# A graph kernel with an LSTM over windows: six pieces of the last layer write into the other stream's F bank

## What is computed

```python
def _L0_gnn_ref(x, adj, Wg0, bg0, Wg1, bg1, Wih, Whh, bih, bhh):
    h = relu(einsum('ts,bsh->bth', adj, x @ Wg0 + bg0))
    h = relu(einsum('ts,bsh->bth', adj, h @ Wg1 + bg1))
    for p in range(1, 5):
        nw = T // p
        last = _lstm_last(Wih[p-1], Whh[p-1], bih[p-1], bhh[p-1], h[:, :nw*p].reshape(B*nw, p, H))
        h = h.at[:, arange(nw)*p + p-1, :].set(last.reshape(B, nw, H))
    return h

def _L1_gnn_ref(x, W, adj, bias):
    h = einsum('bjf,kfo->kbjo', x, W)
    return adj_diag @ h[0] + adj_upper @ h[1] + adj_lower @ h[2] + bias

h = maximum(layernorm(x), 0);  x = x + _L0_gnn_ref(h, adj, ...)
h = maximum(layernorm(x), 0);  x = x + _L1_gnn_ref(h, W, adj, bias)
```

## Time and profile before

| | |
|---|---|
| median of three runs | 401.27 us (401.26 to 401.31) |
| span of the profiled execution, first to last instruction | 399.1 us |
| what lies around the span, against the median | 2.2 us |
| busy: TensorE, its weight loads | 393.3 us, 345.3 us |
| busy: VectorE, ScalarE, GpSimd | 346.5 us, 287.4 us, 44.0 us |
| granted TensorE clock | 1.000 over the span |

### The profile page before, as it was taken

One profiled execution on the slowest core, in us unless ns is written; L12 is line 12 of the kernel. 1 busy time (PEld: TensorE's weight loads), 2 busy tenths in 40 slices (PEclk: granted clock), 3 DMA queues, 4 the chain that ended last, 5 costly groups with the idle time before them and its releaser, 6 DMA issues.

```text
span 399.1 us, 6598 instructions
## 1 busy us (share of the span) xinstructions
PE 393.3 (99%) x2394; PEld 345.3 (87%) x2394; DVE 346.5 (87%) x886; ACT 287.4 (72%) x579; POOL 44.0 (11%) x44
## 2 busy tenths in 40 slices
PE   8999999999999999999999999999999999999997
PEld 7787889998987789899877879899797788989886
DVE  6569999998998998887998898988898979787897
ACT  4668777875897777777689676777589677767554
POOL 4910200100300003000110000300020000000250
PEclk9999999999999999999999999999999999999999
DMA  7830000000000000000000000000000000000003
GB/s 205 315 140 2 0 0 2 2 0 2 0 1 2 26 28 0 28 2 1 2 16 10 28 0 29 0 28 1 2 2 26 0 28 26 2 26 3 0 0 133
DMA packets 5503, 11.18 MB, mean 28 GB/s; under 512 B 1120, under 2 KB 2528, under 8 KB 4960
## 3 DMA queue, kind: packets, MB, share of 16 engines
q1 hardware_dynamic: 5472, 10.77, 7.5%
HBM read 6.57 MB, written 4.19 MB: 27 GB/s over the span
## 4 chain that ended last, share of the span: by engine, by line
PE 79%; DVE 14%; ACT 4%; issue 1%; DMA 1%; POOL 0%; SPq 0%; DVEq 0%; ACTq 0%
PE PS L549 11%; PE PS L540 11%; PE PS L541 10%; PE PS L572 6%; PE PS L569 6%; PE PS L568 6%; PE PS L615 5%; PE PS L490 4%; PE PS L480 4%; PE PS L472 4%; PE PS L457 3%; PE PS L607 3%; PE PS L608 3%; PE PS L609 3%; ACT GT L869 2%; PE PS L582 1%
## 5 line engine op out<-in xcount | busy, mean ns | idle before, releaser
L869 ACT ACTIVATE GT<-PS,BG 128x256 f32<-128x256 f32 (+2 forms) x312 | 157.9, 563 | 17.5 <-PE PS L572 12.8
L540 PE MATMUL PS<-HH,WIH 128*128 128x256 f32 (+2 forms) x312 | 107.2, 344 | 0.1
L541 PE MATMUL PS<-HH,WIL 128*128 128x256 f32 (+2 forms) x312 | 102.7, 330 | 0.0
L549 PE MATMUL PS<-HL,WIH 128*128 128x256 f32 (+2 forms) x294 | 97.3, 331 | 0.6
L884 ACT ACTIVATE TC<-CS 128x512 f32<-128x512 f32 (+2 forms) x88 | 44.9, 510 | 43.6 <-DVE CS L1014 32.5
L387 POOL TENSOR_TENSOR RS<-VE,NHALF 128x4 f32<-128x4 f32 (+2 forms) x18 | 29.9, 1661 | 344.5 <-DVE VE L950 263.9
L540 PEld LDWEIGHTS PS<-HH,WIH 128*128 128x128 f32 x312 | 58.8, 188 | 9.3 <-DVE HH L1052 4.3
L541 PEld LDWEIGHTS PS<-HH,WIL 128*128 128x128 f32 x312 | 58.9, 189 | 3.9 <-issue 1.2
L549 PEld LDWEIGHTS PS<-HL,WIH 128*128 128x128 f32 x294 | 55.5, 189 | 6.6 <-DVE HL L1060 2.4
L572 PE MATMUL PS<-SL,WHH 128*128 128x256 f32 (+2 forms) x192 | 60.1, 313 | 0.2
L568 PE MATMUL PS<-SH,WHH 128*128 128x256 f32 (+2 forms) x192 | 59.9, 312 | 0.0
(11 more groups left out here) (95 smaller groups left out, 655.5 us busy)
## 6 DMA issues: line engine op xcount, KB each, us to landing
out_tbd<-X SPq DMA_DIRECT2D x15, 256.0 KB, 2.0
X<-x_tbd SPq DMA_DIRECT2D x3, 1024.0 KB, 12.9
WI<-wih_t SPq DMA_DIRECT2D x1, 1024.0 KB, 5.2
X<-x_tbd SPq DMA_DIRECT2D x3, 256.0 KB, 3.7
WH<-whh_t SPq DMA_DIRECT2D x1, 768.0 KB, 6.6
X<-x_tbd SPq DMA_DIRECT2D x2, 128.0 KB, 2.4
WL<-w_l SPq DMA_DIRECT2D x1, 192.0 KB, 6.4
WG<-wg SPq DMA_DIRECT2D x2, 64.0 KB, 2.8
```

What stands on the lines that cost most here:

```text
L540: pe.matmul(dst, WIH[:, p - 1, cols], x_high, start=True, stop=False)
L541: pe.matmul(dst, WIL[:, p - 1, cols], x_high, start=False, stop=False)
L549: mm = pe.matmul(dst, WIH[:, p - 1, cols], x_low, start=False, stop=(j == 0))
L869: act.activation(GT[:, s, q, 0:n], bank(s, q)[:, 0:n], ACT.Tanh if q == C else ACT.Sigmoid, bias=BG[:, 4 * (p - 1) + q:4 * (p - 1) + q + 1 ...
```

## The change

Six pieces change their bank: value 1, value 3 and quad 0's sum go from stream 0's F bank to stream 1's, and value 2, quad 1's turn and value 4 from stream 1's to stream 0's. Each piece, and the F gate of unit 6, then waits for the reader of what its new bank held before.

```diff
-         (2, 2): (Piece(VALUE, 0, 1, (TURN, 0)),), (3, 0): (Piece(VALUE, 1, 0, (SUM, -1)),),
-         (3, 2): (Piece(VALUE, 2, 1, (VALUE, 0)),), (4, 0): (Piece(VALUE, 3, 0, (VALUE, 1)),),
-         (4, 1): (Piece(TURN, 1, 1, (VALUE, 2)),), (4, 3): (Piece(SUM, 0, 0, (VALUE, 3)),),
-         (5, 1): (Piece(VALUE, 4, 1, (TURN, 1)),), (6, 1): (Piece(VALUE, 5, 1, (VALUE, 4)),),
+         (2, 2): (Piece(VALUE, 0, 1, (TURN, 0)),), (3, 0): (Piece(VALUE, 1, 1, (VALUE, 0)),),
+         (3, 2): (Piece(VALUE, 2, 0, (SUM, -1)),), (4, 0): (Piece(VALUE, 3, 1, (VALUE, 1)),),
+         (4, 1): (Piece(TURN, 1, 0, (VALUE, 2)),), (4, 3): (Piece(SUM, 0, 1, (VALUE, 3)),),
+         (5, 1): (Piece(VALUE, 4, 0, (TURN, 1)),), (6, 1): (Piece(VALUE, 5, 1, (SUM, 0)),),
-START_F = {6: (SUM, 0), 7: (VALUE, 6), 10: (VALUE, 8), 11: (VALUE, 9), 12: (VALUE, 10), 13: (VALUE, 11)}
+START_F = {6: (VALUE, 4), 7: (VALUE, 6), 10: (VALUE, 8), 11: (VALUE, 9), 12: (VALUE, 10), 13: (VALUE, 11)}
```

## The result

| | before | after |
|---|---|---|
| median of four runs beside each other | 401.26 us (401.23 to 401.31) | 405.72 us (405.61 to 405.87) |
| span of the profiled execution | 399.1 us | 403.6 us |
| ratio of the times | | 1.011, interval 1.0096 to 1.0123 |

A forecast was written before the change was run, and what follows sets the result against it. TensorE, busy 393.3 of 399.1 us, was taken to bound the kernel; 1.64 + 1.31 + 1.31 us in three groups made 4.26, a span of 403.4, and with 2.2 for the runs' median 405.5 us, range 404.3 to 407.0.

The forecast's parts named there:

- Value 1: Value 1 now waits for ScalarE's copy of value 0: cost 0.33 us in group 2, 1.31 in group 1.
- Values 2 and 3, turn 1, quad 0's sum, value 4 at no cost: These pieces get no later reader to wait for in their new banks, so they were costed at zero.
- Value 5, groups 2 and 3: Value 5 waits for VectorE's add of quad 0's sum, behind unit 5's cell: TensorE 1.31 us late, everything included.
- Group 1: New stops at values 1 and 5, less old stops and one wait that vanish: the group ends 1.64 us late.
- The old stop at unit 4: Group 1's 0.37 us stop at unit 4 vanishes and absorbs 0.28, leaving TensorE 1.03 us late.
- the removed wait at unit 6's F gate: Group 1: the gate no longer waits for the add; it loaded at 125.54, the queue would have allowed 125.46.
- The rule weighed: If TensorE's reorder window took a stopped load ahead of its wait, each of six stops would be about 0.1 us shorter.
- The swallowed stop: Value 1's stop is swallowed before unit 5, so only value 5's counts: sum 3.06, 404.3 us; chance 0.07.
- the full lateness: ScalarE and VectorE fall behind by TensorE's whole lateness in group 1, stops give nothing back: 407.0 us; chance 0.06.
- The clock: Each new stop is followed by unit 6 at 1.2 GHz instead of 2.4: 13.5 us more, 419 us; chance 0.02.
- Not slower: Lateness is absorbed behind value 6, where TensorE already waits for an engine that didn't move: 401.2 us; chance 0.03.
- The sign that both engines' idle before unit 6's gates grows: In the changed profile, ScalarE's and VectorE's idle before unit 6's gates grows; before it was 0.80 and 1.23 us.

The follow-up runs named there:

- the two single waits: Kernel before, banks kept, one wait added each: value 1 also for value 0's copy, 402.67 us; value 5 also for the add of quad 0's sum, 404.73 us.
- the pair: Kernel before, banks kept, with both added waits, value 1's for value 0's copy and value 5's for quad 0's add: 406.12 us.

## Why the prediction was right

405.5 us was forecast and 405.72 measured, an added time of 4.26 against 4.46 us. Point by point:

- *What bounds the kernel.* TensorE's queue, without slack. The stretch table carries 4.44 us into a span longer by 4.5; the two single waits add up to the pair within 0.01 us in the medians and 0.17 us in the stretches.
- *Value 1.* Forecast were a load at 113.97 in group 1 and one 0.45 late in group 2. The first came at 113.97, the second with a bracket of 0.50 (0.45 late and 0.04 of the queue's own gap). Right.
- *Values 2 and 3, turn 1, quad 0's sum, value 4 at no cost.* None has a bracket in any group. Right. One reading was wrong without effect: value 3 waits for value 1's copy before and after, so its wait didn't change at all.
- *Value 5, groups 2 and 3.* 1.31 us late each was forecast, 1.31 and 1.30 measured. The step that needed most care, that the add is itself carried along with TensorE's lateness, holds: VectorE's cell now waits 0.15 us for ScalarE's gate and starts at once when it comes.
- *Group 1.* 1.64 was forecast and 1.83 measured: the one mis-sized term. Of the 0.19, 0.11 is value 5's load (1.95 late against 1.84) and 0.08 the F gate. The old stop at unit 4 absorbed 0.21 and not 0.28 (behind value 1 TensorE was 1.34 late, behind turn 1 1.13): before, the work behind that stop had given back 0.12 and not the 0.05 I counted. The stop at value 4 absorbed 0.28 and not 0.30, so TensorE was 0.86 late in unit 5 and not 0.73, and the add ended at 126.13 and not 126.03. And the removed wait at unit 6's F gate, counted as 0.08, was worth 0.01: before, value 6 loaded 0.62 behind the F gate, now 0.69 behind it, so the queue had already given that short stop back. I had priced it without the 0.12 us that I allowed every other stop.
- *The rule weighed.* By a reorder window that takes a waiting load ahead of its wait the sum would have been 3.7. The loads in the trace start 0.05 us behind their releaser, never ahead of it. The Trainium skill's sentence ("TensorE: Matmul & The Clock Gate", section "Architectural detail") speaks of loads pulled ahead of running matmuls; where the load itself waits, no run here shows that.
- *The rivals.* The swallowed stop (404.3) and the full lateness (407.0) are both off by over a microsecond. The clock stayed at 1.000, so stops of 1.1 to 1.5 us don't touch it here. "Not slower" fell on the idle rows it was judged by: ScalarE's wait of 0.80 us for unit 6 is unchanged. The sign that both engines' idle before unit 6's gates grows came true for VectorE (1.23 to 2.20); ScalarE's grew ahead of value 5's copy instead (none before, 0.82 now, group 2).

## What to carry to other kernels

When a buffer changes hands, ask of each user who its new predecessor's reader is and where that reader stands in its own engine's order; here a wait for an add behind the next unit's cell costs 1.0 us at one piece and nothing at the next. On an engine without slack such a stop goes to the end in full, so it can be priced from two times, the releaser's end and the waiter's slot, less what the queue gives back. And before a stop is removed, look for the next wait on the same engine behind it: it may only be hidden by the first. When a step moves ahead of a cell, follow the cell too: here the delay was free behind units 5 and 9 and cost 0.25 us behind unit 4.

## What the runs showed that was not expected

- A load behind two waits, where one was added, started some 0.06 us later than behind the last wait alone (brackets of 0.56 for 0.50, and 1.21 for 1.14), and the profile then names "issue" in place of the engine waited for. Why is not shown.
- The new stops (brackets of 0.50 to 1.50 us) gave back 0.11 or 0.12 us (value 1 in group 1: the load was 1.45 late, the next piece of work 1.34). Two short stops did not follow that: one of 0.08 us gave back nearly all of itself, and value 9's of 0.29 us gave back 0.07.
